# Next batch row's first two units of attention scores issued inside the feed-forward's last steps, with their maxima in a buffer of their own

## What is computed

```python
h = _layernorm(x) * (1 + ca) + sa
x = x + ga * attn_block(h)              # RMS norm, 32 heads of 8, rope, W_o, then silu-gated MLP
h = _layernorm(x) * (1 + cb) + sb
x = x + gb * ffn(h)
# attention: four blocks of 128 positions, causal inside a block
attn = where(causal | other_block, floor, q @ k.T * 8 ** -0.5); attn = softmax(attn)
# ffn
base_out = (silu(gate_base) * up_base) @ Wd.T
for e in experts:                       # weight we is zero for all but the two picked
    g_lora = xf @ Ag_e.T @ Bg_e.T * 2; u_lora = xf @ Au_e.T @ Bu_e.T * 2
    hh = silu(gate_base + g_lora) * (up_base + u_lora)
    acc += (hh @ Ad_e.T @ Bd_e.T * 2) * we[:, None]
out = base_out + acc
```

## Time and profile before

| what | us |
|---|---|
| median of 3 runs | 748.44 |
| lowest, highest | 746.32, 748.56 |
| the profiled execution, its own time | 751.13 |
| its span, first to last instruction | 749.3 |
| PE busy in the span | 652.2 (87%) |
| DVE busy | 410.3 (55%) |
| ACT busy | 321.6 (43%) |
| POOL busy | 193.5 (26%) |

### The profile page before, as it was taken

How to read it: one execution, slowest core, us unless ns; L and a number is a source line. 1 busy time by engine, 2 the same in 40 slices (tenths; PEclk the granted TensorE clock), 3 DMA queues, 4 the chain that set the end, 5 groups by cost and what they waited for, 6 DMA issues and landing times.

```text
span 749.3 us, 14252 instructions
## 1 busy us (share of the span) xinstructions
PE 652.2 (87%) x5640; PEld 436.0 (58%) x5640; DVE 410.3 (55%) x617; ACT 321.6 (43%) x472; POOL 193.5 (26%) x268
## 2 busy tenths in 40 slices
PE   4860899899899899899899899899899999878996
PEld 2740356666686365566686356566686466636672
DVE  1562456367745556367845656367745555346554
ACT  3341245626534145635634235626534244425441
POOL 2032575103201464102301474103201476000000
PEclk9585599999999699999999899999999799997997
DMA  8245010002402010001402010002402100000000
GB/s 334 77 151 141 20 59 3 2 1 57 114 1 56 30 58 3 2 1 46 124 0 55 31 58 3 2 1 54 116 1 56 57 2 2 1 1 1 1 0 29
DMA packets 16475, 32.77 MB, mean 44 GB/s; under 512 B 5280, under 2 KB 5920, under 8 KB 16160
## 3 DMA queue, kind: packets, MB, share of 16 engines
q1 hardware_dynamic: 14880, 28.74, 12.9%
q0 software_dynamic: 1536, 3.15, 1.6%
HBM read 12.99 MB, written 2.10 MB: 20 GB/s over the span
## 4 chain that ended last, share of the span: by engine, by line
PE 67%; DVE 9%; SPq 8%; ACT 7%; issue 5%; DMA 3%; DVEq 0%; POOL 0%; ACTq 0%; POOLq 0%
PE bank L1229 8%; PE bank L1401 7%; SPq L390 7%; PE bank L1336 7%; PE bank L1231 7%; PE bank L1230 7%; PE bank L1465 4%; PE bank L1353 3%; PE bank L1379 3%; PE bank L1545 3%; PE bank L1363 3%; PE bank L1547 2%; PE bank L1546 2%; PE bank L1251 2%; PE bank L1600 2%
## 5 line engine op out<-in xcount | busy, mean ns | idle before, releaser
L970 DVE TENSOR_REDUCE arena<-bank 128x8 f32<-128x1024 f32 x64 | 78.1, 1223 | 86.4 <-PE bank L1353 86.2
L1336 PE MATMUL bank<-mask 128*128 128x512 bf16 x256 | 85.1, 417 | 29.6 <-POOL k_wide L500 26.0
L1229 PE MATMUL bank<-n_hi,w_lo 128*128 128x512 f32 x200 | 87.1, 435 | 11.2 <-DVE n_lo L1025 6.0
L1161 DVE TENSOR_TENSOR arena<-arena,bank 128x512 f32<-128x512 f32 (+1 forms) x72 | 49.1, 687 | 82.8 <-ACT arena L755 82.4
L755 ACT ACTIVATE arena<-bank 128x512 f32<-128x512 f32 (+1 forms) x72 | 42.5, 596 | 102.4 <-PE bank L1547 53.2
L1230 PE MATMUL bank<-n_lo,w_hi 128*128 128x512 f32 x200 | 80.9, 404 | 0.0
L1231 PE MATMUL bank<-n_hi,w_hi 128*128 128x512 f32 x200 | 80.8, 404 | 0.0
L705 ACT ACTIVATE tile_f<-bank 128x1024 f32<-128x1024 f32 x64 | 64.2, 1022 | 38.3 <-PE bank L1379 38.2
L500 POOL TENSOR_TENSOR k_wide<-n_lo,head_of 128x512 fp32r<-128x512 f32 x32 | 33.0, 1036 | 155.9 <-PE bank L1547 142.3
L689 ACT CAST q_st<-bank 4x512 fp32r<-4x512 f32 x32 | 18.5, 578 | 116.1 <-PE bank L1363 116.1
L520 POOL TENSOR_SCALAR arena_r<-q_st,const 100x512 fp32r<-100x512 f32 x96 | 64.8, 690 | 0.2
(11 more groups left out here) (157 smaller groups left out, 1238.4 us busy)
## 6 DMA issues: line engine op xcount, KB each, us to landing
q_st<-arena_r SPq DMA_DIRECT2D x96, 64.0 KB, 2.0
k_st<-arena_r SPq DMA_DIRECT2D x48, 64.0 KB, 2.9
k_st<-arena_r POOLq DMA_DIRECT2D x48, 64.0 KB, 2.7
h_next<-in_x SPq DMA_DIRECT2D x4, 512.0 KB, 3.8
tile_f<-in_x SPq DMA_DIRECT2D x4, 512.0 KB, 4.9
out<-arena SPq DMA_DIRECT2D x4, 512.0 KB, 2.7
arena<-in_wmod SPq DMA_DIRECT2D x1, 1536.0 KB, 10.1
n_hi<-q_st SPq DMA_DIRECT2D x24, 64.0 KB, 2.0
```

The lines of the kernel that those rows point to most:

```text
L970: nc.vector.tensor_reduce(neg_max[:, 2 * a:2 * a + 2, MROW:KS], slot(("s1", n)).rearrange("p a (h s) -> p a h s", s=P), AX_X, ALU.max, neg ...
L1161: nc.vector.tensor_tensor(pair_tmp[n % 2][0:width], silu_out[n % 2][0:width], up, ALU.mult)\
L1229: nc.tensor.matmul(to, wl[rows, w_cols], ah[rows], start=start, stop=False)
L1336: nc.tensor.matmul(to, mask[:, 0, :], mask[:, which:which + 1, :].broadcast_to([P, GH, P]), start=True, stop=False)
```

## The change

- `neg_max` becomes a tensor of its own (2 KB per partition).
- PE, at the end of a row that is not the last: `s1` 0 stands between the last gate product and `down(5,0)`, `s1` 1 between `down(5,0)` and `down(5,1)`. After `down(5,2)` come `t` 0, `s1` 2 and `s1` 3, and only then line 1600. The next row begins with `t` 1. The two `s1` in the tail wait for the `ff_prod` that frees banks (2, 3) and (4, 5).
- The first six fills use slots 0 and 1 alone (banks 2 to 5), so that banks 0 and 1 stay with the experts' sums: `s1` 3 now waits for ACT's copy of `t` 0. The ring of three restarts with `s2` 0 in slot 2 (banks 0 and 1).
- DVE takes the maxima of unit 0 ahead of the two line-1188 products, and those of unit 1 after their sum, ahead of the last residual step. Before, unit 0 came after the sum and unit 1 in the next row.
- SP fetches the k part of each half ahead of the q part (`highs_back` in the order 1, 0, 3, 2).
- POOL does `v_ex` first and then `k_wide`, without the wait for `gu_ready` 18.
- Ahead of the row loop `t` 0, `s1` 2 and 3 and the maxima of unit 1 are issued too, for row 0.

```diff
+        neg_max = sb("neg_max", [P, GQ, P])
...
-        neg_max = arena[:, 9, :].rearrange("p (g c) -> p g c", c=P)
...
-        fills = []
-        for u in range(AHEAD):
-            fills += [("s1", 2 * u), ("s1", 2 * u + 1), ("t", u)]
+        fills = [("s1", 0), ("s1", 1), ("t", 0), ("s1", 2), ("s1", 3), ("t", 1)]
+        slot_of = dict(zip(fills, (0, 1, 0, 1, 0, 1)))
...
-        slot_of = {fill: n % 3 for n, fill in enumerate(fills)}
+        for n, what in enumerate(fills[6:]):
+            slot_of[what] = (n + 2) % 3
...
-                    for i in range(4):
+                    for i in (1, 0, 3, 2):
                         highs_back(i, row, 1)
...
                 pool.wait_ge(rope_lo.sem, rope_lo.count(row, 4, ahead))
-                if ahead:
-
-                    pool.wait_ge(gu_ready.sem, gu_ready.count(row, FT * VARIANTS))
+                spread_values(row, 0, ahead)
                 for u in range(2):
                     spread_keys(row, u, ahead)
-                spread_values(row, 0, ahead)
...
-                unit_max(row, 1, 0)
                 for u in range(UNITS):
...
+                if not is_last:
+                    unit_max(row, 0, 1)
                 for k in range(2):
                     dve.wait_ge(z_ready.sem, z_ready.count(row, k + 1))
...
                 if not is_last:
-
-                    dve.wait_ge(z_steps.sem, z_steps.count(row, 2))
-                    unit_max(row, 0, 1)
+                    unit_max(row, 1, 1)
...
-                if at >= 3:
-                    what, k = fills[at - 3]
-                    pe.wait_ge(freed_by[what].sem, freed_by[what].count(row, k + 1))
+                before = [f for f in fills[:at] if slot_of[f] == slot_of[(kind, n)]]
+                if before:
+                    what, k = before[-1]
+                    pe.wait_ge(freed_by[what].sem, freed_by[what].count(row, k + 1, ahead))
...
+            def second_scores_for_max(row, ahead):
+
+                max_transposed(row, 0, ahead)
+                for a in range(2):
+                    scores_for_max(row, 2 + a, ahead)
+
...
-                max_transposed(0)
-                for a in range(2):
-                    scores_for_max(row, 2 + a, 0)
-                max_transposed(1)
+                max_transposed(row, 1, 0)
...
                 lora(FT - 1, 2)
+                if not is_last:
+
+                    pe.wait_ge(ff_prod.sem, ff_prod.count(row, FF_STEPS.index((FT - 2, 2)) + 1))
+                    scores_for_max(row, 0, 1)
                 down(FT - 1, 0)
+                if not is_last:
+
+                    pe.wait_ge(ff_prod.sem, ff_prod.count(row, len(FF_STEPS)))
+                    scores_for_max(row, 1, 1)
                 down(FT - 1, 1)
                 down(FT - 1, 2)
                 if not is_last:
-
-                    scores_for_max(row, 0, 1)
-                    scores_for_max(row, 1, 1)
+                    second_scores_for_max(row, 1)
```

More of the change, by code:

```diff
@@ L964, in unit_max @@
                 if u:
-                    dve.wait_ge(max_t.sem, max_t.count(row, u))
+                    dve.wait_ge(max_t.sem, max_t.count(row, u, ahead))
                 for a in range(2):
@@ L1219, in _ @@
             unit_max(0, 0, 0)
+            unit_max(0, 1, 0)
             with dve.Fori(0, B - 1) as row:
@@ L1325, in front_projections, with fill @@
                 project_v(1)
-            def fill(row, kind, n):
+            def fill(row, kind, n, ahead):
                 at = fills.index((kind, n))
-                if at >= 3:
-                    what, k = fills[at - 3]
-                    pe.wait_ge(freed_by[what].sem, freed_by[what].count(row, k + 1))
+                before = [f for f in fills[:at] if slot_of[f] == slot_of[(kind, n)]]
+                if before:
+                    what, k = before[-1]
+                    pe.wait_ge(freed_by[what].sem, freed_by[what].count(row, k + 1, ahead))
                 return slot((kind, n))
@@ L1347, in scores_for_max @@
                         pe.wait_ge(tile.sem, tile.count(row, GQ * 16, ahead))
-                to = fill(row, "s1", n)
+                to = fill(row, "s1", n, ahead)
                 for g in range(2):
@@ L1355, in scores_for_max, with max_transposed @@
                 last.then_inc(s1_ready.sem, 1)
-            def row_steps(row, is_last):
[L1359 to L1364, removed]
+            def max_transposed(row, u, ahead):
+                pe.wait_ge(max_done.sem, max_done.count(row, 2 * u + 2, ahead))
+                to = fill(row, "t", u, ahead)
+                for gq in range(GQ):
+                    last = nc.tensor.transpose(to[0:KS, 0, gq * P:(gq + 1) * P], neg_max[:, gq, 0:KS], con("ident"))
+                last.then_inc(max_t.sem, 1)
+            def second_scores_for_max(row, ahead):
+                max_transposed(row, 0, ahead)
+                for a in range(2):
+                    scores_for_max(row, 2 + a, ahead)
+            def row_steps(row, is_last):
                 def shifted_scores(n):
@@ L1373, in shifted_scores @@
                             half_stacked(pe, row, half, 0)
-                    to = fill(row, "s2", n)
+                    to = fill(row, "s2", n, 0)
                     for g in range(2):
@@ L1417, in row_steps @@
                     if u + AHEAD < UNITS:
-                        max_transposed(u + AHEAD)
+                        max_transposed(row, u + AHEAD, 0)
                     if not is_last:
@@ L1633, in _ @@
             scores_for_max(0, 1, 0)
+            second_scores_for_max(0, 0)
             pe.wait_ge(plain_loaded.sem, 9 * 16)
```

## The result

| | median us | lowest, highest | runs |
|---|---|---|---|
| before | 747.38 | 745.80, 748.56 | 4 |
| changed | 727.22 | 726.71, 728.69 | 4 |

The ratio is 0.9735, with a 95% interval of 0.9708 to 0.9762: 20 us faster. The forecast was 727.1. The profiled execution of the changed kernel took 727.33 us, its span is 725.5, 23.8 less than the span before.

The account below looks back on a forecast made before the run. PE bounds attention; row boundaries lose time to low clock and a chain waiting on itself. Three boundaries at 14.7 us, 44.1 against 65.44, save 21.3: 748.44 - 21.3 = 727.1 us, range 724.4 to 736.

Parts of the forecast that it names:

- The sum: Three row boundaries: 14.3 + 0.4 = 14.7 us each, 44.1 in all against 65.44, a gain of 21.3 us.
- the collision: Ahead of T: the early `k_wide` meets two `ff_low` on DVE and costs 0.4 us per boundary, bounds 0 and 0.76.
- `t` 0: PE at a boundary, after `down(5,2)`: runs from 5.45 to 5.92 us after T.
- DVE's sum: DVE at a boundary: the experts' sum runs from 6.56 to 7.25 us after T, 1.0 later than before but hidden.
- POOL's spread: POOL at a boundary: query spread could start at 6.75 us after T, goes at 7.25, ends at 10.37.
- line 1600: PE at a boundary, after `s1` 3: 7.86 to 9.65 us after T, priced at 1.79, other end 3.57.
- The store and the exponentials: Boundary covers: first exponential ends at 12.6, before 13.3; store of `out` lands at 13.8, before `normalise` at 16.
- The step that was missing: PE at the jump into the next row: `t` 1 from 9.67 to 10.14 us after T with almost no gap.
- Rival 1: Boundaries: low clock stays in part; half of 30.8 low us costs 7.7 us, giving 734.8; chance 0.22 in various sizes.
- Rival 2: Boundaries: POOL takes the shared port ahead of DVE's sum, 0.95 us later each, 2.9 in all, 730.0; chance 0.15.
- Rivals 3: Boundaries: no effect, something not late now (q fetch, store) gives back 19 us or more, about 748; chance 0.04.
- Rival 4: Boundaries: slower, PE runs them whole at 1.2 GHz, 25.1 us each, 9.9 more than now, 758.3; chance 0.03.

Follow-up runs that it names:

- early_k_wide: The kernel before with only the change's GpSimd and SyncE part: k fetched first, v_ex first, k_wide without the wait for the last gate product; 743.77 us, ratio 0.9951.
- q_first: The changed kernel with SyncE's old fetch order, q ahead of k for each half; 727.13 us, ratio 0.9746 to the kernel before.
- k_wide_late: The changed kernel with GpSimd's wait for the last gate product put back ahead of k_wide; 736.68 us, ratio 0.9885 to the kernel before.
- scores_behind_down: The changed kernel with `s1` 0 and 1 moved back behind the last `down`; 741.14 us, ratio 0.9929 to the kernel before.
- filled_gaps: The kernel before with useless matmuls in TensorE's row-boundary gaps, six ahead of down(5,1) and seven ahead of `t` 1; 737.99 us, ratio 0.9884.

## Why the prediction was right, point by point

**The sum.** 14.3 us from T (the first instruction behind the last gate product) and 0.4 ahead of it were forecast for each boundary, 44.1 in all and a gain of 21.3. Measured from T: 15.61, 15.29 and 14.19, a gain of 20.3 us, less 0.4 us ahead of T. The two profiles differ by 2.3 us more in the prologue, which is no part of it. By the medians the gain is 747.38 - 727.22 = 20.2 us, 1.1 less than forecast. That the median lands within 0.2 us of 727.1 is luck: the sum was taken off 748.44, which lies 1.1 above the median of the four executions, and this cancels the 1.1 us by which the gain was too high. The sum missed 2.9 us of jumps, overstated the collision by 0.8 and the rest of a boundary by a little (14.3 us against 14.1 to 14.2 where no jump gap stands).

**Steps that held.** Counted from T = 236.47, first the forecast, then the trace: `t` 0 at 5.45 and 5.40, DVE's sum at 6.56 and 6.49, maxima of unit 1 at 7.2 and 7.10, POOL's spread ready at 6.75 and 6.73, line 1600 at 7.86 and 7.79. Line 1600 (now 1607) was priced at 1.79 at the full clock, far from the other bound of 3.57; it took 1.83 in the third boundary, from 568.40 to the start of `t` 1 at 570.23. The store and the exponentials stayed covered.

**The step that was missing.** "PE's `t` 1 runs from 9.67 to 10.14 with almost no gap" failed in two of three boundaries: it ran at 11.39 and 11.07, and at 9.62 in the third. The sum costed the jump back of the loop at nothing, since in the kernel before `t` 0 follows line 1600 without a gap. There line 1600 took 3.57 us at the low clock and covered it; at the full clock 1.8 us don't. The last wait ahead of the jump is DVE's sum: from its end to the first matmul behind the jump are 247.86 - 243.65 = 4.2 us here. This is a cover that goes when the clock comes back, and the forecast priced the clock but not what the low clock had hidden. The written-out loop shows it, and so do the two boundaries of `early_k_wide`.

**A term that was mis-sized.** 0.4 us for the collision of the early `k_wide` with `ff_low`; measured 0.14. From SyncE's first fetch to T it was 239.16 - 231.30 = 7.86 us and is 236.47 - 228.48 = 7.99. The collision is there (1.38 and 1.48 us above), but less of it reaches TensorE than I estimated. Before, TensorE had 0.16 us of idle of its own ahead of the last gate products (the one at 237.33 is followed at 237.72); that is gone now, so part of the delay fell into it. `q_first`, without the collision, takes 7.87 again (231.40 to 239.27).

**The rivals.** Rival 1, part of the low clock stays, didn't happen in the changed kernel. But `k_wide_late` and `scores_behind_down` show how near it was: one gap of 1.4 us, or 0.6 and 1.56 us in two places, brings it back in one of the three boundaries of a profiled execution. So its chance of 0.22 was not too high for the mechanism. Rival 2, the port: DVE's sum came first by 0.24 us, and POOL's instruction took 1.35 us from 243.20 instead of 1.04. It ended 0.90 behind the end of DVE's sum (243.65), so GpSimd lost 0.31, on the side that was forecast. By the rule named there (the Trainium skill, SBUF — State Buffer, section "SBUF: two separate sides": an exclusive lock, the loser waits in full) the late side should have waited the 0.45 us until DVE's end; it lost 0.31, less than that, and what makes up the rest isn't shown. Rivals 3 and 4 found no support: no new wait gave the gain back, and TensorE ran no boundary at 1.2 GHz. Rival 4's sum held `down` for as long at the low clock as at the full one, since its weights would pace it. The third boundary of `k_wide_late` shows otherwise: there its matmuls start 0.73 us apart (570.47, 571.20, 571.92, 572.64) instead of 0.43, so that rival would have cost 2.4 us more a boundary.

**What the prediction did not say.** The change is three moves that need each other. Without DVE's early maxima 18 of the 20 us go, without the scores between the `down` 14, without the early `k_wide` 9; fetching k first is worth nothing. These losses add up to more than the gain. In part that is because a move that opens a gap also pays for the clock (7.6 us in one boundary of `k_wide_late` against 1.2 in the others), in part because all three lie on one chain.

## What to carry to other kernels

A gap on TensorE has two prices, its own length and the half-speed stretch that may follow; put real work into it first, and where there is none, matmuls of no use can pay (9 us gained here in the old order, 6 in the last row). When an order is priced at full-clock durations, look at what the slow stretch had been hiding, a loop's jump back above all: write the loop out on that one engine, or keep a wait that is resolved late well away from the jump (not tried here). And judge the parts of a reordering by taking each out of the whole, since their values alone (3.7 us for the GpSimd and SyncE part in the old kernel, 9 in the new) say little.

## What the runs showed of the hardware that was not expected

- From the end of the last wait ahead of the jump back of TensorE's loop (DVE's sum) to the first matmul behind it go about 4 us: 247.86 - 243.65 = 4.2 and 409.81 - 405.92 = 3.9 here, and 3.7 to 4.2 wherever such an "issue" gap stands in the other profiles (`filled_gaps`, `early_k_wide`, `k_wide_late`, `q_first`, `scores_behind_down`). With less work than that queued behind the wait, the engine stands: 1.61 and 1.29 us. The third boundary, where the loop is left, has no gap.
- Two boundaries of one execution, with the same instructions, took 17.96 us at the full clock and 22.65 at 0.70 (`early_k_wide`). After the same gap of 1.40 us the clock fell in one of three boundaries of `k_wide_late` and held in two. The four executions of the changed kernel lie within 2.0 us, those of `q_first` within 4.2, and those of the kernel before, where the clock falls at the boundaries, within 11 (744.05 to 755.12).
- The start of the first scores varied by 1.9 us between the two profiled executions (75.18 and 73.31) with the same instructions ahead of them: 0.8 from the first DMA, the rest from when the full clock came.
- The column of the granted clock can mislead where TensorE is thinly used: one stretch of the prologue took 14.22 us at a shown 0.50 and 14.22 at a shown 1.00.
